# Additive attention: TensorE's order without products on constants, a group's sums over two tiles, its loop behind the first tile

## The reference, cut to what matters

```python
q = X @ Wq.T; k = X @ Wk.T; Vy = X @ Wy_w.T + Wy_b
# rho(x) = sqrt(relu(x) + 1e-8) - sqrt(relu(-x) + 1e-8)
e = relu(rho(q[:, :, None, :] + k[:, None, :, :]))      # [B, i, j, A]
scores = einsum('bija,a->bij', e, Wphi)
ex = exp(scores - max_j(scores)); denom = sum_j(ex)
part1 = einsum('bij,bjc->bic', ex, Vy)
Ew = einsum('bij,bija->bia', ex, e)
part2 = Ew @ We_w.T + We_b * denom
out = (part1 + part2) / (denom + 1e-9)
x = x + ga * out
```

## Time and profile before

| What | us |
|---|---|
| median of 3 runs | 6358.82 |
| lowest and highest of these | 6352.87, 6371.05 |
| the profiled execution's own time | 6362.64 |
| its span, first to last instruction | 6361.0 |

### The profile page before, as it was taken

The page is one execution under the profiler, slowest core; times in us unless marked ns, Lnnn a source line. Parts: engine busy times, 40 slices in busy tenths (PEclk is TensorE's granted clock), DMA queues, the critical chain, the costliest instruction groups (busy, mean ns, idle before and its releaser), DMA issues. The chain is left out here.

```text
span 6361.0 us, 94446 instructions
## 1 busy us (share of the span) xinstructions
PE 5456.7 (86%) x32440; PEld 2935.0 (46%) x32440; DVE 4300.9 (68%) x6797; ACT 3707.0 (58%) x2416; POOL 2980.0 (47%) x2483
## 2 busy tenths in 40 slices
PE   5776867579966999999999999999999999859999
PEld 2322323257732444444444444444444444437777
DVE  2857658443334888888888888888888998842221
ACT  1011110210026888888888888988889999634443
POOL 1423425001104666666666665666666666423333
PEclk9988989789987989999999998999999999979999
DMA  1000000000011000000000000000000000010000
GB/s 74 0 0 0 0 0 0 31 3 10 10 68 38 3 3 4 3 5 15 3 5 3 5 3 16 3 3 4 3 11 2 3 2 3 15 68 14 13 13 7
DMA packets 37486, 74.30 MB, mean 12 GB/s; under 512 B 4592, under 2 KB 22224, under 8 KB 34384
## 3 DMA queue, kind: packets, MB, share of 16 engines
q1 hardware_dynamic: 35024, 62.60, 2.8%
q0 software_dynamic: 2176, 7.34, 0.3%
HBM read 50.00 MB, written 19.92 MB: 11 GB/s over the span
## 5 line engine op out<-in xcount | busy, mean ns | idle before, releaser
L802 DVE CUSTOM_DVE_ANT_0 e_slots<-e_slots,banks 128x1024 f32<-128x1024 f32 x2048 | 2474.1, 1218 | 505.8 <-PE banks L529 489.1
L589 ACT ACTIVATE e_slots<-e_slots,eps_rho 128x4096 f32<-128x4096 f32 x512 | 1893.0, 3710 | 103.2 <-POOL e_slots L657 76.3
L529 PE MATMUL banks<-ex_parts,sel 128*128 128x512 f32 x4096 | 1488.3, 446 | 162.4 <-DVE ew L802 81.0
L651 POOL TENSOR_SCALAR e_slots<-k,qt 128x1024 f32<-128x1024 f32 x896 | 1002.8, 1120 | 1067.4 <-DVE ew L802 1002.3
L485 PE MATMUL banks<-e_slots,w_score 128*32 128x256 f32 x16384 | 1397.8, 416 | 107.9 <-ACT e_slots L589 107.9
L580 ACT ACTIVATE e_slots<-k,qt 128x1024 f32<-128x1024 f32 x768 | 860.8, 1143 | 321.0 <-DVE ew L802 316.3
L657 POOL TENSOR_SCALAR e_slots<-e_slots,qt 128x1024 f32<-128x1024 f32 x896 | 1016.0, 1141 | 64.5 <-POOL e_slots L651 25.7
L529 PEld LDWEIGHTS banks<-ex_parts,sel 128*128 128x128 f32 x4096 | 666.5, 202 | 507.5 <-issue 282.7
L485 PEld LDWEIGHTS banks<-e_slots,w_score 128*32 128x32 f32 x16384 | 335.0, 111 | 872.9 <-issue 753.7
L495 PE MATMUL banks<-sel 128*128 128x256 f32 x2112 | 533.0, 334 | 0.0
L495 PEld LDWEIGHTS banks<-sel 128*128 128x128 f32 x2112 | 314.5, 188 | 432.6 <-issue 432.0
(11 more groups left out here) (272 smaller groups left out, 6799.5 us busy)
## 6 DMA issues: line engine op xcount, KB each, us to landing
stage<-in_h SPq DMA_DIRECT2D x8, 1024.0 KB, 4.8
x_tokens<-in_x SPq DMA_DIRECT2D x1, 4096.0 KB, 17.3
w_down<-in_w_down SPq DMA_DIRECT2D x1, 4096.0 KB, 12.3
x_between<-x_tokens SPq DMA_DIRECT2D x8, 512.0 KB, 3.1
kx<-x_between SPq DMA_DIRECT2D x8, 512.0 KB, 4.6
v_all<-v_out POOLq DMA_DIRECT2D x8, 512.0 KB, 3.2
vy<-v_all SPq DMA_DIRECT2D x4, 1024.0 KB, 5.0
xg<-x_between SPq DMA_DIRECT2D x32, 128.0 KB, 2.5
```

Source lines behind the costliest of these rows:

```text
L529: ins = nc.tensor.matmul(spread[n % 2][:, half * W:(half + 1) * W], c_["sel"][:, half, n, :], ex_parts[:, par, :], start=True, stop=True)
L589: nc.scalar.activation(e_slots[:, par, four, :], e_slots[:, par, four, :], ACT.Sqrt, bias=eps_rho[:, 0:1]).then_inc(sqrt_done, 1)
L651: nc.gpsimd.tensor_scalar(e_slots[:, par, n, :], k2[:, :], FLT_MAX, qt[:, par, 1, place(n):place(n) + 1], ALU.min, ALU.max).then_inc(z_cla ...
L802: nc.vector.tensor_tensor_reduce(out=e, in0=e, in1=spread[n % 2], scale=1.0, scalar=0.0, op0=ALU.mult, op1=ALU.add, accum_out=ew[:, q, pla ...
```

## The change

- `keep_clock` and its calls are gone.
- `sums` does one product in a turn instead of two. The first 12 of a group stand in turns 4 to 15 of tile 3, the other 12 in turns 0 to 11 of tile 0 of the next group. `sums_of_e` stands between them, and the last of the 24 tells VectorE (`out_mm`).
- In tile 0 the turned exponentials (the eight short products) move from turn 1 to turn 13, and VectorE's copy of them from turn 2 to turn 14 (`EXT_AT_FIRST`).
- `group_end` part 0 moves to turn 13 of tile 0, part 1 to turn 14, parts 2 and 3 behind turn 15, ahead of the z products.
- TensorE's loop body is in the order tiles 1, 2, 3, 0, with the first tile of all ahead of the loops; the last group has tiles 1 to 3 written out and the last 12 sums behind them.
- The partner's maximum (`swapped_max`) lies in the last column of PSUM bank 6, no longer in SBUF.
- The square root takes its bias as a number, not from the tile `eps_rho`.

```diff
-    EXT_AT, MAX_AT, END_AT = 1, 8, {2: 0, 3: 1, 14: 2, 15: 3}
+    EXT_AT, EXT_AT_FIRST, MAX_AT, END_AT = 1, 13, 8, {14: (1,), 15: (2, 3)}
+    SUMS_AT = 4
-    IDLE_AT, IDLE_PRODUCTS = range(5, 16), 2
...
+        swapped_max = banks[:, 6, W - 1:W]
...
+            def sums(tg, i):
+                if i == 0:
                     pe.wait_ge(out_read, tg + 1)
                     pe.wait_ge(ext_copied, tg * GT + GT + 1)
+                k, j = divmod(i, JT)
+                w = ones[:, :] if k == 0 else vy[:, j, (k - 1) * P:k * P]
+                ins = nc.tensor.matmul(banks[:, 7, k * P:(k + 1) * P], w, ex_t[:, j, :, :].rearrange("p a i -> p (a i)"),
+                                       start=i == 0, stop=True, skip_group_check=True)
+                if i == N_SUMS - 1:
+                    ins.then_inc(out_mm, 1)
...
+            def tile(t, q, last=False, sums_of=None, values=None, more_sums_of=None):
...
+                    if n == (EXT_AT if q else EXT_AT_FIRST):
...
+                    if sums_of is not None and n >= SUMS_AT:
+                        if n == SUMS_AT:
+                            pe.wait_ge(vy_loaded, values)
+                        sums(sums_of, n - SUMS_AT)
+                    if more_sums_of is not None and NP - SUMS_AT + n < N_SUMS:
+                        sums(more_sums_of, NP - SUMS_AT + n)
+
+            def group_on(tg, values, last=False):
+                for q in (1, 2, 3):
+                    tile(tg * GT + q, q, last, tg if q == GT - 1 else None, values)
                 sums_of_e(tg)
+                if not last:
+                    tile(tg * GT + GT, 0, more_sums_of=tg)
+                else:
+                    for i in range(NP - SUMS_AT, N_SUMS):
+                        sums(tg, i)
...
-                                     ACT.Sqrt, bias=eps_rho[:, 0:1]).then_inc(sqrt_done, 1)
+                                     ACT.Sqrt, bias=EPS_RHO).then_inc(sqrt_done, 1)
...
-                    nc.vector.stream_shuffle(half_max[:, 1:2], half_max[:, 0:1],
+                    nc.vector.stream_shuffle(swapped_max, half_max[:, 0:1],
...
+                    if ends is not None and n == EXT_AT_FIRST:
+                        group_end(ends, 0)
-                    if n == EXT_AT + 1:
+                    if n == (EXT_AT if q else EXT_AT_FIRST) + 1:
...
+                    if ends is not None and n > EXT_AT_FIRST:
+                        for k in END_AT[n]:
+                            group_end(ends, k)
                     if queries is not None:
                         for m in Z_AFTER.get(n, ()):
                             z(t + 2, par, m, t * NP)
-                    if ends is not None and n in END_AT:
-                        group_end(ends, END_AT[n])
```

More of the change, by code:

```diff
@@ L515, in sums_of_e @@
                     for i in range(2):
-                        ins = nc.tensor.matmul(banks[:, 7, (k + 1) * P + i:(k + 2) * P:2],
-                                               c_["we2"][:, i, k * P:(k + 1) * P],
-                                               ew[:, :, :].rearrange("p a n -> p (a n)"),
-                                               start=False, stop=True, skip_group_check=True)
-                ins.then_inc(out_mm, 1)
-            def group(tg, values, last):
-                for q in range(GT):
-                    t, par = tg * GT + q, q % 2
-                    pe.wait_ge(parts_done, t + 1 + 1)
-                    for n in range(NP):
-                        pe.wait_ge(xb_freed, t * NP + (n + 1))
-                        for half in range(2):
-                            ins = nc.tensor.matmul(spread[n % 2][:, half * W:(half + 1) * W], c_["sel"][:, half, n, :],
-                                                   ex_parts[:, par, :], start=True, stop=True)
-                        ins.then_inc(bc_done, 1)
-                        if n == EXT_AT:
-                            pe.wait_ge(ext_copied, t + 1)
-                            for j in range(JT):
-                                half, block = divmod(j, JT // BPB)
-                                ins = nc.tensor.matmul(banks[:, 6, j * TI:(j + 1) * TI],
@@ new lines, in sums_of_e @@
+                        nc.tensor.matmul(banks[:, 7, (k + 1) * P + i:(k + 2) * P:2],
+                                         c_["we2"][:, i, k * P:(k + 1) * P],
+                                         ew[:, :, :].rearrange("p a n -> p (a n)"),
+                                         start=False, stop=True, skip_group_check=True)
+            def tile(t, q, last=False, sums_of=None, values=None, more_sums_of=None):
+                par = q % 2
+                pe.wait_ge(parts_done, t + 1 + 1)
+                for n in range(NP):
+                    pe.wait_ge(xb_freed, t * NP + (n + 1))
+                    for half in range(2):
+                        ins = nc.tensor.matmul(spread[n % 2][:, half * W:(half + 1) * W], c_["sel"][:, half, n, :],
+                                               ex_parts[:, par, :], start=True, stop=True)
+                    if n == (EXT_AT if q else EXT_AT_FIRST):
+                        pe.wait_ge(ext_copied, t + 1)
+                        for j in range(JT):
+                            half, block = divmod(j, JT // BPB)
+                            turned_ = nc.tensor.matmul(banks[:, 6, j * TI:(j + 1) * TI],
@@ L549, in group @@
-                sums_of_e(tg)
+                        turned_.then_inc(ext_mm, 1)
+                    ins.then_inc(bc_done, 1)
+                    ahead, m = SCORES_AT[n]
+                    if not (last and q >= GT - ahead):
+                        scores(t + ahead, m, (q + ahead) % 2)
+                    if sums_of is not None and n >= SUMS_AT:
+                        if n == SUMS_AT:
+                            pe.wait_ge(vy_loaded, values)
+                        sums(sums_of, n - SUMS_AT)
```

34 lines of the change are left out of this document (7 added, 27 removed).

## The result

| | before | after |
|---|---|---|
| median, us | 6355.84 (6349.35 to 6371.05, 4 runs) | 6197.74 (6189.22 to 6202.95, 4 runs) |
| profiled execution, us | 6362.6, span 6361.0 | 6189.2, span 6187.5 |
| phase C, first turn to last, us | 2014.5 to 5550.7 = 3536 | 2015.8 to 5375.6 = 3360 |

The changed kernel takes 0.9747 of the time before, 95% interval 0.9725 to 0.9768: 158 us less, where 255 were forecast. The time lies in the range given, but inside rival C (6145 to 6325) and not in the forecast's own stretch (6055 to 6145).

The account below looks back on a forecast made before the run. ScalarE and TensorE with VectorE were taken to bind together; 29.0 + 24.4 + 24.4 + 25.0 = 102.8 us a group saves 233 + 23 + 3 = 259 us, giving 6100 us, range 5995 to 6225.

Parts of the forecast that it names:

- rival C: Longer falls of TensorE's clock in tiles 1, 2 and 3: a group of 104.5 to 110 us, 6145 to 6325; chance 0.18.
- Bounds: Two limits meet in a tile: ScalarE at 24.3 us, and TensorE's turns of 1.23 or 1.48 us with VectorE.
- The loop is turned: TensorE's stop at the loop's branch is covered behind tile 0 or removed: 6.4 us a group in batches 0 to 2.
- The extra products go: TensorE saves 2.7 us a tile; tiles 1 and 2 go to 24.4 us, clock falls mostly hidden behind ScalarE.
- Sums: Twelve sums leave tile 3, 27.6 to 25.0 us; in tile 0 they add 2.6 where extra products take off 2.7.
- Tile 0: The group's end in later turns adds 1.2 us and the short products 0.3: 27.5 to 29.0 us.
- Bias of the square root: ScalarE's square root with a constant bias: taken as 0, with 0.1 us either way a call as bounds.
- Last group: The one group without a next one, at the stage's end: a gain of 3 us.
- D: Without filler TensorE stays at 1.2 GHz for most of a tile: 134 us a group, 7070 us; chance 0.08.
- E: TensorE's stop for instructions stays uncovered, 6165 us, or moves to batch 3 as well; chance 0.07.
- A: The forecast itself: a group of 101 to 104.5 us, 6055 to 6145 us; chance 0.50.
- B: ScalarE alone binds: a group of 97.3 to 101 us, 5929 to 6055 us; chance 0.17.

Follow-up runs that it names:

- e2: The kernel before with TensorE's loop turned round behind tile 0 and nothing else, extra products kept: 6215.0 us.
- e4: The changed kernel with products on a constant added in turn 1 of tiles 1 to 3, where TensorE waits: 6090.4 us.
- e9: The changed kernel with the extra products back in turns 5 to 15 of tiles 1 and 2, and the partner's maximum in SBUF: 6165.4 us.
- e3: The kernel before with 80 and 56 tiny products set once ahead of its two loops, moving them in TensorE's program: 6232.9 us.
- e1: The kernel before without TensorE's extra products on constants, nothing else changed: 6236.3 us.
- e11: The changed kernel with all 24 sums of a group back in tile 3, two per turn from turn 4: 6209.9 us.
- e10: The kernel of e4 with 16 more products on constants ahead of tile 1's first turn: 6123.3 us.

## Why the prediction was right, and where it was not

**Bounds.** Right: ScalarE and the turns of TensorE with VectorE meet. A tile 2 at full clock takes 23.96 us, which is the floor of 24.3 less four times the 0.09 us that the square root got shorter.

**The loop is turned, 6.4 us a group, "either way".** Right, and both ways occurred. In the changed kernel the stop is gone; in e2's second loop, e4 and e9 it is there and covered. The prediction gave the removal only as an aside (132 instructions shorter). It was the largest single gain: e3 got 137 us from the place of the code alone, and some 160 without its padding.

**The extra products go.** This step failed: it took what TensorE's clock would cost as hidden. It said of a fall: "Added to 21.8 or 23.4 one fall still stays near 24.3, so it is mostly hidden behind ScalarE". Tiles 1 and 2 took 25.39 and 25.36 us, not 24.4. What the runs showed in its place: TensorE's waits for the other engines at a tile's start are long (2.83 us in the row above, 1.17 in the earlier trace rows), the lower clock then lasts several turns of 2.16 us, not one of 1.92, and it comes in tiles 1, 2 and 3 of most groups. Tile 1 had a fall in every group before, too; what grew is that tile 2 has one in 25 of 32 groups, where it had one in 17 before and 11 in e3. Removing the products lost some 20 to 30 us in the old order (e1 against e3 without its padding) and 28 in the new one (e9), and filling the waits that come before the falls gained 103 us (e4). With them filled, the groups take 102.4, where 102.8 was forecast, and the kernel takes 6090, where 6100 was. That closeness is partly luck: it has the gain of the bias below in it, which the forecast put at 0.

**Sums.** Tile 3 at full clock is 25.14 us, as forecast (25.0); its falls make the mean 26.25. In tile 0 the twelve sums were to cost 2.6 us and the extra products that leave to give 2.7. By e11 the sums cost 1.9, by e3 and e1 (27.75 to 27.25) the products gave 0.5. So the spreading was worth 12 us at most, which the intervals don't separate from nothing.

**Tile 0.** 28.15 us, where 29.0 was forecast. The group's end in turns 13 to 15 was put at +1.5 us. But e11's tile 0, which has it and no sums, takes 26.2 us, 1.0 less than e1's 27.25, of which the square root's bias may be 0.36. By this comparison the sign of the term was wrong: the sum charged parts 0 and 1 at their new place and took nothing off at the old one, though VectorE's wait there was 0.61 us and the parts cost 1.25. It hid that the removal gave only 0.5.

**Bias of the square root.** Mis-sized: 0 was taken, 0.1 us a call was the bound, and 0.09 was measured. Undone, it costs 51 us. This gain and the unforeseen falls partly cancel; without it the changed kernel (6248) would be no better than before without its extra products (6236), and 33 us slower than before with its loop turned and nothing else (e2, 6215).

**Maximum in PSUM.** 0, as said.

**Last group.** A gain of 3 was forecast; from the first turn of its tile 0 to the end of the stage it took 5375.6 - 5278.9 = 96.7 us, 4.6 more than before. TensorE's clock was at 1.00 in its last two tiles before and is at 0.73 now; tile 2 of them by stretches, before and after:

```profile
5512.00:5532.10 20.10, 17.41 (x116) 9.25 (x116) 19.61 (x39) 6.16 (x4) 2.00 (x2) 1.00 0.00 1
...
5331.80:5354.70 22.90, 19.45 (x94) 7.29 (x94) 20.10 (x38) 6.68 (x4) 1.97 (x2) 0.73 0.00 1
```

Behind its last turn twelve sums now stand alone, 4.32 us, and VectorE's copy waits 5.56 us for them, where it waited 1.20:

```profile
5376.83 4.32 PE L502 MATMUL banks<-ex_t,vy 128*128 128x128 f32 x24
```

In terms of the sum: batches 0 to 2 gave 24 x (112.5 - 105.4) = 170, batch 3 gave 7 x (106.1 - 104.6) = 11, the last group took 5 and the rest of the program 3, together 173, as 6362.6 - 6189.2. The medians lie 158 apart. The rivals: D (the clock stays down) was far from it, E's stop came back only in other kernels, covered but for e10, and C was the mechanism that held, at its lower end.

**Range and chances.** Two figures of the prediction don't follow from its own sum. With 31 groups, 101 to 104.5 us make 6045 to 6155, not 6055 to 6145, and A, E, half of B and half of C add up to 0.75, where the range was called 8 in 10. Neither changes how the measured time is read: it is C's.

What stays open: why the three z products take 4.07 us. From 2150 to 4450 us one takes 883 to 942 ns in the kernels with extra products in TensorE's turns (before, e3, e2, e9) and 1087 to 1155 in all others; e1 moved it by taking these products out and nothing else. What in them does it isn't shown.

## What to carry to other kernels

Count the packets of the instruction queue inside a loop: when each pass fetches again, a few dozen tiny instructions ahead of the loop can be worth more than any order within it, though they cost their own time when they stand on the path (some 25 us here), and a branch set beside another engine's long work hides most of the stop. Products that only keep the clock bring most where TensorE waits (103 us), less in turns that it binds (28 us), and they cost between a branch that fetches and the first product that others need (33 us). A constant bias, 0.09 us a call, is worth its price times the calls and more where the engine sets the floor.

## What was not expected of the hardware

- On TensorE the same body of 1678 instructions is fetched anew in every pass (208 more packets of about 16 KB over 24 passes) when it begins at instruction 2101 or 4162, and never when it begins at 2261, 2481, 3782 or 4054.
- A square root of 128x4096 takes 3617 to 3620 ns with a constant bias and 3707 to 3710 with one from SBUF.
- The minimum over one column takes 148 to 155 ns in all 128 calls with its second operand in PSUM, and 154 to 965, median 580, with both in SBUF.
- TensorE's clock at 0.99 instead of 0.98 went with a slower kernel (e10 against e4): the clock by itself is no measure.
